# Three cross-attentions: full 32-bit products ahead of the scores in a step, and a tile's values in one block over two banks

## The reference

```python
# L0 and L2: 16 heads of 64 (the "wide" ones)
q = (x @ w_q).reshape(B, Sq, HEADS, DIM_HEAD).transpose(0, 2, 1, 3)
k = (context @ w_k).reshape(B, Skv, HEADS, DIM_HEAD).transpose(0, 2, 1, 3)
v = (context @ w_v).reshape(B, Skv, HEADS, DIM_HEAD).transpose(0, 2, 1, 3)
sim = jnp.einsum('bhid,bhjd->bhij', q, k) * SCALE
attn = jax.nn.softmax(sim, axis=-1)
out = jnp.einsum('bhij,bhjd->bhid', attn, v)
return out @ w_o + b_o
# L1: 16 heads of 16, with biases on q, k and v, and attn = jnp.clip(attn, -CLAMP, CLAMP) ahead of the softmax
```

## Time and profile before

| | us |
|---|---|
| runs, three | 2016.35, 2022.66, 2028.9 (median 2022.66) |
| profiled execution, its time | 2018.47 |
| its span, from the first to the last instruction | 2016.6 |
| TensorE busy in the span | 1633.3 (81%) |
| VectorE / ScalarE / GpSimd busy | 1173.3 / 867.7 / 711.4 |

### The profile page before, as it was taken

How to read it: one execution, slowest core, us unless ns; L and a number is a source line. 1 busy time by engine, 2 the same in 40 slices (tenths; PEclk the granted TensorE clock), 3 DMA queues, 4 the chain that set the end, 5 groups by cost and what they waited for, 6 DMA issues and landing times. The chain is left out here.

```text
span 2016.6 us, 36051 instructions
## 1 busy us (share of the span) xinstructions
PE 1633.3 (81%) x12690; PEld 1402.0 (70%) x12690; DVE 1173.3 (58%) x3187; ACT 867.7 (43%) x2475; POOL 711.4 (35%) x780
## 2 busy tenths in 40 slices
PE   6999998650785999977999999699595388757996
PEld 6988997330465999946899889456494266546996
DVE  5666665688774888835666666289413565442222
ACT  4666664114543888812666666200131133112332
POOL 7655552541116999713000000177312211112111
PEclk9999999885896999987999999799697588858998
DMA  8444441010004333205222222520362210931112
GB/s 249 149 148 148 149 148 67 29 39 5 0 1 132 130 134 133 94 16 169 75 93 93 93 93 75 165 95 1 91 202 62 68 52 28 320 119 56 38 38 81
DMA packets 120795, 195.52 MB, mean 97 GB/s; under 512 B 17672, under 2 KB 87408, under 8 KB 120272
## 3 DMA queue, kind: packets, MB, share of 16 engines
q1 hardware_dynamic: 113504, 181.32, 27.3%
q0 software_dynamic: 3408, 8.54, 1.2%
q10 hardware_dynamic: 3712, 3.41, 0.6%
HBM read 154.16 MB, written 45.52 MB: 99 GB/s over the span
## 5 line engine op out<-in xcount | busy, mean ns | idle before, releaser
L672 DVE TENSOR_SCALAR xattn_oT<-bank,xattn_last 128x256 f32<-128x256 f32 x256 | 111.7, 478 | 100.1 <-PE bank L512 100.1
L592 ACT ACTIVATE xattn_probs<-bank,xattn_negmax 128x257 f32<-128x257 f32 x256 | 124.2, 485 | 57.8 <-DVE xattn_negmax L653 57.8
L653 DVE TENSOR_REDUCE xattn_negmax<-bank 128x1 f32<-128x257 f32 x256 | 108.0, 422 | 63.0 <-PE bank L485 61.3
L597 ACT ACTIVATE xattn_probs<-xattn_probs,xattn_rsum 128x257 f32<-128x257 f32 x256 | 131.9, 515 | 1.4 <-DVE xattn_rsum L657 1.4
L832 POOL TENSOR_SCALAR xattn_probs<-xattn_probs,xattn_rsum 128x257 f32<-128x257 f32 x128 | 119.9, 937 | 22.9 <-DVE xattn_rsum L1067 22.7
L1907 POOL MEMSET scan_decay<- 128x64 f32 x1 | 0.2, 214 | 337.1 <-POOLq L51 337.1
L603 ACT CAST xattn_probsT_hi<-bank 128x256 fp32r<-128x256 f32 x256 | 95.7, 374 | 40.4 <-PE bank L492 36.7
L662 DVE TENSOR_TENSOR xattn_probsT_lo<-bank,xattn_probsT_hi 128x256 fp32r<-128x256 f32 x256 | 104.9, 410 | 8.3 <-ACT xattn_probsT_hi L603 7.2
L492 PE MATMUL bank<-ident,xattn_probs 128*128 128x128 f32 x512 | 103.6, 285 | 2.5 <-ACT xattn_probs L597 2.0
L136 PE MATMUL bank<-ident,xn 128*128 128x128 f32 x144 | 32.6, 406 | 90.0 <-DVE xn L112 90.0
L481 PE MATMUL bank<-xattn_ctxT,xattn_qk_hi 128*128 128x258 f32 x256 | 93.6, 366 | 0.5 <-DVE xattn_qk L649 0.5
(11 more groups left out here) (500 smaller groups left out, 5426.1 us busy)
## 6 DMA issues: line engine op xcount, KB each, us to landing
xattn_ctxT<-ctx_partsT SPq DMA_DIRECT2D x64, 516.0 KB, 3.6
xattn_ctxN<-ctx_partsN SPq DMA_DIRECT2D x64, 384.0 KB, 3.1
ctx_partsT<-xattn_ctxT SPq DMA_DIRECT2D x32, 516.0 KB, 3.0
moe_w<-in_L_ffn_W SPq DMA_DIRECT2D x16, 1024.0 KB, 13.9
ctx_partsN<-xattn_ctxN SPq DMA_DIRECT2D x32, 384.0 KB, 3.9
moecap_w_early<-in_L_ffn_w SPq DMA_DIRECT2D x10, 1024.0 KB, 12.7
xattn_rawN<-in_ctx SPq DMA_DIRECT2D x32, 192.0 KB
moecap_w_late<-in_L_ffn_w SPq DMA_DIRECT2D x6, 1024.0 KB, 7.5
```

Source lines behind the costliest of these rows:

```text
L592: nc.scalar.activation(probs[:, n % RING, :], SB[n % 2][:, 0:KV], ACT.Exp, bias=negmax[:, n % RING:n % RING + 1], accum_out=psum[:, n % RI ...
L597: nc.scalar.mul(probs[:, n % RING, :], probs[:, n % RING, :], rsum[:, n % RING:n % RING + 1]).then_inc(norm_ready, 1)
L653: nc.vector.tensor_reduce(negmax[:, n % RING:n % RING + 1], SB[n % 2][:, 0:KV], AX.X, ALU.max, negate=True).then_inc(negmax_ready, 1)
L672: nc.vector.tensor_scalar(oT[k][:, heads, b, :], by_head(OB[:, k * 2 * P:(k + 1) * 2 * P]), last[:, k, j * PER_TILE + b:j * PER_TILE + b + ...
```

## The change

In all three stages TensorE's full 32-bit products (queries, folds, values, project) are moved ahead of the scores in their step; they stood behind them (and behind the keys). A tile's values are made in one block in step 7, instead of four blocks in steps 6 to 9 (two, in 6 and 8, in the clipped stage). In the wide stages the two halves go to two banks, M2 and M0, with their own semaphore; in the clipped stage they go to two halves of M2. ScalarE copies both halves in step 8. Two waits are new: the second half of the values waits until M0's first fold of the tile has been read, and the second fold waits until M0's values have been copied.

```diff
--- before.py
+++ after.py
@@ -249,7 +249,7 @@
     SPLIT = 10
     PIECES = 4
     FOLD = (4, 10, 12, 14)
-    VALUES = (6, 7, 8, 9)
+    VALUES, TAKE = 7, 8
     PROJECT = {11: range(0, 3), 13: range(3, 6), 15: range(6, 8)}
     M_FILLS, M_START = 1 + GROUPS, 3
     with ExitStack() as ctx:
@@ -296,9 +296,10 @@
         turned = st.sem("turned")
         probsT_hi_ready, probsT_ready = st.sem("probsT_hi_ready"), st.sem("probsT_ready")
         pv_done, oT_ready = st.sem("pv_done"), st.sem("oT_ready")
-        aT_ready, x_done = st.sem("aT_ready"), st.sem("x_done")
+        values_done, aT_ready, x_done = st.sem("values_done"), st.sem("aT_ready"), st.sem("x_done")
         banks = [b[:, :] for b in core.bank]
         SB, TB, (OB, M0, M1, M2) = banks[0:2], banks[2:4], banks[4:8]
+        VALUE_BANKS = (M2, M0)
         START = [(M0, M1), (SB[0], SB[1]), (OB, M2), (M0, M1)]
         block = ctx.enter_context(nc.Block())
 
@@ -456,6 +457,8 @@
                     pe.wait_ge(qk_ready, folds(j, g - 1, 1) + 1)
                 elif g == 3:
                     pe.wait_ge(qk_ready, folds(0, 0, 1) + 1)
+                if g == 1 and j >= 2:
+                    pe.wait_ge(aT_ready, (j - 1) * 2)
                 for k in range(GROUP):
                     for odd, bank in enumerate(fold_banks(j, g)):
                         h = g // 2 * 8 + odd + 2 * k
@@ -512,24 +515,22 @@
                     mm = nc.tensor.matmul(OB[:, 2 * P:4 * P], second(c), lo[:, c], start=False, stop=(c == 1))
                 mm.then_inc(pv_done, 1)
 
-            def values(j, part):
-                m = part // 2
-                if part == 0:
-                    pe.wait_ge(wv_loaded, 48)
-                    pe.wait_ge(oT_ready, (j + 1) * UNITS)
-                    if j:
-                        pe.wait_ge(x_done, j)
-                elif part == 2:
-                    pe.wait_ge(aT_ready, j * 2 + 1)
-                for k in range(part % 2 * 2, part % 2 * 2 + 2):
-                    for v, o in [(wv1, oT[0]), (wv2, oT[1])]:
-                        for c in range(2):
-                            h = (m * QM + k) * 2 + c
-                            mm = nc.tensor.matmul(M2[c * HD:(c + 1) * HD, k * P:(k + 1) * P], v[:, h * HD:(h + 1) * HD],
-                                                  o[:, group_of(h // 8 * 2, h % 2) * GROUP + h % 8 // 2],
-                                                  start=(v is wv1), stop=(v is wv2), tile_position=(0, c * HD))
-                if part % 2:
-                    mm.then_inc(m2_filled, 1)
+            def values(j):
+                pe.wait_ge(wv_loaded, 48)
+                pe.wait_ge(oT_ready, (j + 1) * UNITS)
+                if j:
+                    pe.wait_ge(x_done, j)
+                for m, bank in enumerate(VALUE_BANKS):
+                    if m:
+                        pe.wait_ge(qk_ready, folds(j + 2, 0, 0) + 1 if j + 2 < TILES else folds(TILES - 1, GROUPS - 1, 0) + 1)
+                    for k in range(QM):
+                        for v, o in [(wv1, oT[0]), (wv2, oT[1])]:
+                            for c in range(2):
+                                h = (m * QM + k) * 2 + c
+                                mm = nc.tensor.matmul(bank[c * HD:(c + 1) * HD, k * P:(k + 1) * P], v[:, h * HD:(h + 1) * HD],
+                                                      o[:, group_of(h // 8 * 2, h % 2) * GROUP + h % 8 // 2],
+                                                      start=(v is wv1), stop=(v is wv2), tile_position=(0, c * HD))
+                    mm.then_inc(values_done, 1)
 
             def project(j, chunks):
                 if chunks[0] == 0:
@@ -553,18 +554,18 @@
                 j, s = divmod(t, UNITS)
                 if 0 <= t - TURN < ALL:
                     turn_probs(t - TURN)
-                if t < ALL:
-                    scores(t)
                 if j + 1 < TILES:
                     if s < 4:
                         queries(j + 1, s // 2, range(s % 2 * 2, s % 2 * 2 + 2))
                     if s in FOLD:
                         to_context(j + 1, FOLD.index(s))
                 if j:
-                    if s in VALUES:
-                        values(j - 1, VALUES.index(s))
+                    if s == VALUES:
+                        values(j - 1)
                     if s in PROJECT:
                         project(j - 1, PROJECT[s])
+                if t < ALL:
+                    scores(t)
                 if 0 <= t - PV < ALL and (t - PV) % 2:
                     probs_ctx(t - PV)
 
@@ -604,8 +605,8 @@
                     probsT_hi_ready, 1)
 
             def values(j, m):
-                act.wait_ge(m2_filled, j * 3 + m + 1)
-                nc.scalar.copy(aT[:, m * QM:(m + 1) * QM, :].rearrange("p k n -> p (k n)"), M2).then_inc(aT_ready, 1)
+                act.wait_ge(values_done, j * 2 + m + 1)
+                nc.scalar.copy(aT[:, m * QM:(m + 1) * QM, :].rearrange("p k n -> p (k n)"), VALUE_BANKS[m]).then_inc(aT_ready, 1)
 
             ln.act(act, 0)
             queries(0)
@@ -626,8 +627,9 @@
                     probsT_hi(t - TURN)
                 if ahead and s == 1:
                     queries(j + 1)
-                if behind and s in (7, 9):
-                    values(j - 1, (s - 7) // 2)
+                if behind and s == TAKE:
+                    for m in range(2):
+                        values(j - 1, m)
                 if ahead and s in FOLD:
                     fold_hi(j + 1, FOLD.index(s), 0)
 
@@ -673,7 +675,7 @@
                                             last[:, k, j * PER_TILE + b:j * PER_TILE + b + 1], None, ALU.add).then_inc(oT_ready, 1)
 
             def add(j):
-                dve.wait_ge(m2_filled, j * 3 + 3)
+                dve.wait_ge(m2_filled, j + 1)
                 nc.vector.tensor_tensor(core.x[:, j, :], core.x[:, j, :], M2[:, 0:D], ALU.add).then_inc(x_done, 1)
 
             ln.dve(dve)
@@ -720,7 +722,7 @@
     RING, PAIRS = 4, 3
     EXP, NORM, TURN, PV, OUT = 1, 2, 4, 6, 6
     Q_STEP, Q_TAKE, Q_SPLIT, BLOCKS_AT = 1, 2, 3, 4
-    VALUES, TAKE, PROJECT, ADD = (6, 8), (7, 9), 10, 11
+    VALUES, TAKE, PROJECT, ADD = 7, 8, 10, 11
     BLOCKS = PER_TILE * CD * 2
     with ExitStack() as ctx:
         st = Stage(core, ctx, name)
@@ -924,20 +926,18 @@
                     mm = nc.tensor.matmul(OB[:, 2 * P:4 * P], second(c), lo[:, c], start=False, stop=(c == 1))
                 mm.then_inc(pv_done, 1)
 
-            def values(j, m):
-                if m == 0:
-                    pe.wait_ge(wv_loaded, 64)
-                    pe.wait_ge(oT_ready, (j + 1) * UNITS)
-                    if j:
-                        pe.wait_ge(x_done, j)
-                else:
-                    pe.wait_ge(aT_ready, j * 2 + 1)
-                for i in range(SHARE):
-                    for v, o in [(wv1, oT[0]), (wv2, oT[1])]:
-                        for c in range(0, P, STRIP):
-                            h = m * HPC + c // HD + i
-                            mm = nc.tensor.matmul(M2[c:c + STRIP, 0:P], v[:, h, :], o[:, h, :, :], start=(i == 0 and v is wv1),
-                                                  stop=(i == SHARE - 1 and v is wv2), tile_position=(0, c))
+            def values(j):
+                pe.wait_ge(wv_loaded, 64)
+                pe.wait_ge(oT_ready, (j + 1) * UNITS)
+                if j:
+                    pe.wait_ge(x_done, j)
+                for m in range(CD):
+                    for i in range(SHARE):
+                        for v, o in [(wv1, oT[0]), (wv2, oT[1])]:
+                            for c in range(0, P, STRIP):
+                                h = m * HPC + c // HD + i
+                                mm = nc.tensor.matmul(M2[c:c + STRIP, m * P:(m + 1) * P], v[:, h, :], o[:, h, :, :],
+                                                      start=(i == 0 and v is wv1), stop=(i == SHARE - 1 and v is wv2), tile_position=(0, c))
                 mm.then_inc(m2_filled, 1)
 
             def project(j):
@@ -958,17 +958,17 @@
                 j, s = divmod(t, UNITS)
                 if 0 <= t - TURN < ALL:
                     turn_probs(t - TURN)
+                if j + 1 < TILES and s == Q_STEP:
+                    queries(j + 1)
+                if j:
+                    if s == VALUES:
+                        values(j - 1)
+                    if s == PROJECT:
+                        project(j - 1)
                 if t < ALL:
                     scores(t)
                     if key_step(t):
                         keys(*key_step(t))
-                if j + 1 < TILES and s == Q_STEP:
-                    queries(j + 1)
-                if j:
-                    if s in VALUES:
-                        values(j - 1, VALUES.index(s))
-                    if s == PROJECT:
-                        project(j - 1)
                 if 0 <= t - PV < ALL and (t - PV) % 2:
                     probs_ctx(t - PV)
 
@@ -1012,8 +1012,8 @@
```

(11 more changed lines are left out.)

## The result

The changed kernel took **2032.8 us** (median of five runs, 2029.94 to 2042.6), against 2021.12 for the kernel before in runs on the same chip (2016.35 to 2028.9). The ratio is **1.0063**, 95% interval 1.0034 to 1.0092. Measured twice more, it was 1.0039 [1.0021, 1.0058] and 1.0053 [1.0034, 1.0072]. So the change makes the kernel about half a per cent slower: the forecast was 6 us faster, 2016.7, in a range up to 2031. The case "within 1%" came true, but with the sign reversed, and the median lies 1.8 us outside the range.

A forecast was written before the change was run, and what follows sets the result against it. TensorE, nearly always busy, was taken as the bound. Two wide stages at -2.75 us and the clipped one at -0.5 gave -6: 2012.5 in the profiled execution's time, 2016.7 against the median of the runs, range 2004 to 2031.

The forecast's parts named there:

- 6 x (-0.2) + 0.8 - 1.5 - 0.85 = -2.75: Each wide stage: middle tiles, first tile, last tile and drain added up, 2.75 us saved.
- Q and O use the whole array: nothing: Query and output products on TensorE: moving them ahead of the scores costs 0, as nothing is exposed on either side.
- First tile, no V: +0.8: First tile of a wide stage, which has no values products: 0.8 us slower.
- Middle tile -0.2: Middle tile of a wide stage: switch prices, waits and the merged values block sum to 0.2 us saved.
- the 0.3 at T7: Middle wide tile, transposes of step 7: they wait for the next normalisation, at 6.92 for 6.62 us, +0.3.
- terms 1 and 5: Middle wide tile: values in one block instead of four, -0.96 us; shorter wait for oT before the values start, -0.5.
- terms 2 and 3: Middle wide tile: folds between transposes and scores, +0.2 us; first fold in step 4 waits 1.51 instead of 0.90, +0.6.
- Last tile and drain: End of a wide stage: last tile without folds -1.5 us; drain no longer waits for the first half's copy, -0.85.
- Clipped stage -0.5: Clipped stage: the merged block's gain of about 0.3 a tile is lost waiting for GpSimd's normalisation; only the drain saves 0.5.
- A: Rival: in step 8 ScalarE's two copies delay the softmax chain and hold TensorE at step 10's transposes; 2033 us, 13%.
- B: Rival: the new waits in steps 4 to 7 don't come, as VectorE and ScalarE run ahead; 2003 us, 13%.
- C: Rival: exposed tenths belong to semaphore waits, a merged block saves nothing: 2026, 4%; opposite, switches behind transposes free: 1989, 3%.

The follow-up runs named there:

- first experiment: Changed kernel with scores first again in step 0 of the wide stages and steps 0 and 1 of the clipped one: 2022.4 us, ratio 1.0038.
- second experiment: Changed kernel with scores first in all 16 steps of each stage's first tile: 2023.72 us, ratio 1.0037.
- third experiment: Changed kernel with the old order everywhere, scores ahead of the full products, so only the values in one block remain: 1999.72 us, ratio 0.9922.
- the fourth: Kernel before with the new order alone, values still in four blocks (two in the clipped stage): 2065.25 us, ratio 1.0241.
- sixth experiment: Changed kernel with the tile's first fold in step 5 and not 4: 2012.2 us, ratio 0.9965.
- the seventh: Changed kernel with the old order and the wide stages' values in two blocks, steps 7 and 8 (clipped stage one): 2005.84 us, ratio 0.9934.

## Why the prediction was wrong, step by step

**The step that failed is the sum of a stage: "6 x (-0.2) + 0.8 - 1.5 - 0.85 = -2.75".** It prices the first tile like a middle one without values, and has no term for what tile 0's step 0 waits for. The runs show +3.4 and +3.2 a wide stage. By parts, from S5 to S5 (added up that way the terms come to -2.5 a stage; the -2.75 has the middle tile's -0.16 rounded to -0.2):

- *The start of a stage: +0.65 by the terms (the fold of step 4); measured +3.0 and +3.5.* In step 0 of tile 0, I had priced moving Q ahead of S at nothing ("Q and O use the whole array: nothing"), which is right for the array and leaves out what Q waits for. In a middle tile the queries' bank is free long before. In step 0 of tile 0 it isn't, and the row that would have told it stands in the trace of before: L445 with 1.11 idle, released by xattn_qk of L649, with a group of scores in front of it. The first experiment gave 2.2 us back in either stage, of which 1.6 are the clock. In step 4 the fold's wait is the right mechanism with the wrong size: the 0.6 presumes that the fold waited 0.83 before, as in a middle tile, but tile 0's didn't wait at all. T4 to T5 went from 2.13 to 3.57, +1.44. Together this is the largest piece, 5.1 of the 13.7 us between the forecast -6 and the measured +7.7 for the three stages.
- *"First tile, no V: +0.8": too small.* From S5 to S5 that term is the next tile's fold, 0.6, and 0.2 for the switches; measured +2.1. Tile 0 has neither values nor project to fill its steps, so its later folds come early and wait for VectorE to clear their bank. TensorE, steps 12 and 14 of tile 0 after:

```profile
53.07 0.44 PE L495 MATMUL bank<-ident,xattn_probs 128*128 128x128 f32 x2
54.08 1.16 PE L466 MATMUL bank<-xattn_qT,xattn_wk 64*128 64x128 f32 x16 [0.57 <-DVE xattn_qk L651]
...
58.04 0.44 PE L495 MATMUL bank<-ident,xattn_probs 128*128 128x128 f32 x2
58.54 0.71 PE L466 MATMUL bank<-xattn_qT,xattn_wk 64*128 64x128 f32 x8
```

 The fold of step 12 comes 1.01 behind T12, that of step 14 0.50 behind T14, where 0.31 is the least. Before, the scores stood in this time, and the same fold came 0.98 behind T12 with no idle. The second experiment takes 1.4 us of the first period away.
- *Middle tile -0.2: measured 0.0.* Each event of the timeline above lies within 0.11 us of the forecast (values start at T4 + 7.45 for 7.34). One step has the wrong owner: the 0.3 at T7 belongs to the block and not to the order, for T6 to T7 takes 1.12 us in the third experiment too, where a plain step takes 0.82. The block in the old order made 39.64 (terms 1 and 5 and this 0.3 give 39.74), and the order added 1.25 (terms 2 and 3 and T6's 0.2: 1.0).
- *Last tile and drain.* From the last S5 but one on, the terms give -3.15: -0.8 in the last period (-0.96 - 0.5 + 0.5 + 0.15), then -1.5 and -0.85. Measured -1.6 and -2.5 in the means of the two wide stages (one record of the kernel before has 2.6 us more in the second one's rest than the others). The rest is 1.8 to 2.0 us shorter in the records where it is shortest (45.42 and 45.46, 45.24 and 45.30, for 47.3), with the drain's 0.68 gone as forecast, and so it is in the third experiment (45.36); the last period fell by 0.2 only. Its first light steps are the place: T0 to T5 of the last tile takes 7.33 us (307.81 to 315.14), before 6.85 (302.39 to 309.24), although no product stands there in either kernel. It is the order: the third experiment, with the block and the old order, has 6.84 there, and the fourth, with the order alone, 7.33. That the scores of the steps before come late behind their products, with nothing to cover the softmax chain, I read from the spacing alone.
- *Clipped stage -0.5: measured +1.1.* The five middle periods are +0.2 each (forecast 0), the last one +0.2, start and first period +0.3 and 0.0, the rest -0.4 (forecast -0.5). So the wide stages' fault at the start isn't here: the eight queries of step 1 (1.91 us at 639.10, with a granted clock of 0.57 in the four us around) now stand ahead of that step's scores, but in the next steps TensorE has to wait for GpSimd's normalisations in any case: 1.13 us ahead of one pair of transposes, where the kernel before waits 0.69 and 1.37 us ahead of two. The block alone gives 28.07 us a middle period, the order alone 28.90, both 28.22, for 28.04 before: the block saves 0.7 only of what the order costs. Of these 0.9 us 0.7 lie in step 6, where the first values block now idles 0.50.

Added up against the forecast's own parts: the starts 5.1, the first tiles 2.6, the middle ones 1.6, last tiles and drains 2.3, the clipped stage 1.6, and 0.5 of rounding, or 13.7 us.

The rivals: *A* did not come: T9 to T10 takes 1.96 us in the changed kernel, without a wait, where the forecast has 2.00. *B*, that the new waits don't come, is refuted by L466's idle of 1.44 and by the sixth experiment, in which 1.3 us go with the fold's place. *C*, that a switch has no price of its own, is refuted by the seventh: +0.32 for one more block. With it falls the reading of the rule that I weighed from "TensorE: Matmul & The Clock Gate" of the Trainium skill (Part 2, step 1), as a whole account of such switches: a further block would cost nothing by it. In its opposite form C is refuted as well: the shortest distance from a pair of transposes to a fold in the changed kernel is 0.31 (302.85 to 303.16), as assumed, where scores follow transposes by 0.14.

None of my rivals had the mechanism that decided: all looked at the middle of the stages. The time 2033 of rival A and the measured 2032.8 agree by chance, and so does the middle period, 40.9, with the one before: two halves of 1.3 us cancel.

**What stays open.** The three changed stages are 7.7 us longer, while the whole kernel is 8 to 13 longer. The other nine stages have the same instructions in both kernels; their sums are 1054.4, 1055.6 and 1062.1 us before and 1070.9, 1058.4 and 1060.1 in the changed kernel, 5.8 apart in the mean, and 1052.5 to 1061.6 in the seven experiments. Three records each don't tell this from scatter; whether the changed stages leave something behind that makes the later ones slower isn't settled. The second experiment's median, 7 above its base with its three stages at the level of before, stays open with it.

## What to carry to other kernels

When an instruction is moved ahead of another in a steady loop, look at the first and the last pass on their own: what it waits for there may be the work of the prologue, and what stood in front of it was the cover. A wait read in a middle pass isn't the first pass's: 0.83 us there was none in tile 0, so the same move cost 1.44 and not 0.6. Split a change of two parts before judging it: here merging the blocks was worth -0.8%, the order beside it took 1.3% back, and the merge with the first fold one step later is worth -1.5%. And put a product behind the scores if it may have to wait: here the scores feed the softmax chain of three engines at once, and a late product feeds only the next tile.

The idle of the groups tells of the last point. VectorE's maxima and ScalarE's exponentials, and the folds, in the page after:

```profile
L655 DVE TENSOR_REDUCE xattn_negmax<-bank 128x1 f32<-128x257 f32 x256 | 108.4, 423 | 195.3 <-PE bank L488 193.8
L593 ACT ACTIVATE xattn_probs<-bank,xattn_negmax 128x257 f32<-128x257 f32 x256 | 123.1, 481 | 176.3 <-DVE xattn_negmax L655 176.2
...
L466 PE MATMUL bank<-xattn_qT,xattn_wk 64*128 64x128 f32 x1024 | 73.3, 283 | 25.5 <-DVE xattn_qT L640 20.0
```

The idle before the maxima is 195.3 us (63.0 before) and before the exponentials 176.3 (57.8). Most of this costs nothing, as neither engine is the bound. What costs is TensorE's idle, such as the 20.0 before the folds (10.0 before): 14 waits of some 1.4 us instead of 12 of 0.8, the two new ones being those of tile 0.

## What the runs showed of the hardware

- With an idle of 2.22 us at the start of a wide stage TensorE's granted clock fell to 1.2 GHz in five of six such starts of the same kernel (nine of ten with the fourth and sixth experiments), and stayed at 2.4 in the other; with 1.11 us it fell in none of 16. The fall cost 1.6 us more (15.2 for 13.6), and not in each execution.
- One more change between a block on half of the array's columns and whole-array matmuls cost 0.32 us a tile, both sides together with the transposes it lengthens.
- The nine stages that no kernel here changes vary from 1052.5 to 1070.9 us in sum between profiled executions, 18 us or 0.9% of the kernel's time, more than most effects measured here. Only the lengths of parts between fixed events, which repeat to 0.1 us in the middle of a stage, told the causes apart.
